# Another order of the same steps on five engines, and another assignment of products to three PSUM banks, in an audio tower on one core

## The reference

```
h = patches(x) @ W.T + b                                  # 64 x 92 x 128
q, k, v = split(layernorm(h) @ w_qkv.T)
p = softmax(q @ k.T * 64**-0.5)                           # per head, 92 x 92
a = layernorm_over_heads(einsum('bhij,hg->bgij', p, reattn_w)) * ln_g + ln_b
h = h + concat_heads(a @ v) @ w_out.T + b_out
x = layernorm(h)
c = two largest of softmax(x @ gate_w.T), scaled to sum 1, 0 elsewhere
h = h + sum_e c_e * (relu(x @ w1_e + b1_e) @ w2_e + b2_e) + relu(x @ sw1 + sb1) @ sw2 + sb2
```

## Time and profile before

| | |
|---|---|
| median of 3 runs | 638.89 us (638.68 to 639.09) |
| the profiled execution, its own time | 639.33 us |
| its span | 637.5 us |
| mean granted TensorE clock | 0.981 |
| busy: PE, DVE, ACT, POOL | 606.4, 441.2, 402.4, 368.5 us |
| setup and start, to `dots` 0 of group 0 | 24.4 us |
| iteration 0, iteration 1 | 28.9, 40.5 us |
| iterations 2 to 14 | 467.8 us, 13 of them |
| iteration 15; 16 and 17 | 33.0; 42.9 us |

### The profile page before, as it was taken

How to read it: one execution, slowest core, us unless ns; L and a number is a source line. 1 busy time by engine, 2 the same in 40 slices (tenths; PEclk the granted TensorE clock), 3 DMA queues, 4 the chain that set the end, 5 groups by cost and what they waited for, 6 DMA issues and landing times.

```text
span 637.5 us, 17017 instructions
## 1 busy us (share of the span) xinstructions
PE 606.4 (95%) x6275; PEld 529.2 (83%) x6275; DVE 441.2 (69%) x1322; ACT 402.4 (63%) x1346; POOL 368.5 (58%) x545
## 2 busy tenths in 40 slices
PE   8886889999999999999999999999999999999796
PEld 7775779898889888898889889888888889887674
DVE  5453666768777776868777776867777786867553
ACT  3466557676866667676866667675866667666400
POOL 2566437565674847565674847566683856546300
PEclk9988969999999999999999999999999999999999
DMA  6000030120303030120303021030313020020303
GB/s 231 1 27 4 22 97 25 38 97 2 110 26 108 26 105 29 32 103 1 110 26 108 25 100 35 25 111 1 109 27 108 26 81 28 15 97 2 109 2 119
DMA packets 15460, 37.43 MB, mean 59 GB/s; under 512 B 1809, under 2 KB 4241, under 8 KB 15377
## 3 DMA queue, kind: packets, MB, share of 16 engines
q1 hardware_dynamic: 15376, 36.34, 17.1%
HBM read 33.13 MB, written 3.20 MB: 57 GB/s over the span
## 4 chain that ended last, share of the span: by engine, by line
PE 75%; ACT 7%; DVE 7%; POOL 5%; issue 3%; DMA 1%; SPq 0%; ACTq 0%; POOLq 0%; DVEq 0%
PE ps_fill L414 13%; PE ps_fill L416 11%; PE ps_fill L415 11%; PE ps_mix L642 9%; PE ps_dots L630 9%; PE ps_av L650 7%; PE ps_fill L778 6%; PE ps_fill L570 4%; ACT ex L803 3%; DVE aT L1086 3%; POOL sum L1227 2%; PE ps_fill L770 2%; ACT sq L811 2%; POOL sum L1230 1%; PE ps_fill L761 1%
## 5 line engine op out<-in xcount | busy, mean ns | idle before, releaser
L803 ACT ACTIVATE ex<-ps_dots,negmax 128x92 f32<-128x92 f32 x384 | 123.7, 341 | 7.0 <-DVE negmax L1070 6.5
L1227 POOL TENSOR_TENSOR sum<-sq 92x384 f32<-92x384 f32 x64 | 64.2, 1003 | 80.3 <-ACT sq L811 79.5
L1221 POOL TENSOR_TENSOR probs<-ex,rinv 128x552 f32<-128x552 f32 x64 | 71.0, 1109 | 29.7 <-DVE rinv L1076 29.7
L642 PE MATMUL ps_mix<-mixk,probs 64*92 64x64 f32 x1536 | 79.2, 251 | 5.5 <-DVE aT L1086 5.4
L642 PEld LDWEIGHTS ps_mix<-mixk,probs 64*92 64x92 f32 x1536 | 70.7, 163 | 16.3 <-issue 10.7
L1167 DVE SCALAR_TENSOR_TENSOR act<-ps_fill,b_neg,spread 128x368 f32<-128x368 f32 x123 | 67.9, 591 | 19.9 <-PE ps_fill L416 15.1
L803 ACT ACTIVATION_READ_ACCUMULATOR ex<-ps_dots,negmax 128x1 f32 x384 | 81.4, 212 | 0.0
L630 PE MATMUL ps_dots<-xT,yT 128*64 128x92 f32 x1536 | 75.6, 249 | 5.5 <-ACT ex L803 4.9
L630 PEld LDWEIGHTS ps_dots<-xT,yT 128*64 128x64 f32 x1536 | 65.0, 139 | 11.6 <-ACT ex L803 8.8
L1086 DVE TENSOR_TENSOR aT<-ps_mix,arstd 92x384 f32<-92x384 f32 x128 | 64.9, 547 | 7.1 <-ACT arstd L821 5.2
L1244 POOL TENSOR_TENSOR xT<-xT_split_hi,xT_split_lo 128x368 f32<-128x368 f32 x16 | 15.6, 973 | 86.1 <-DVE xT_split_lo L1146 86.1
(11 more groups left out here) (190 smaller groups left out, 1566.9 us busy)
## 6 DMA issues: line engine op xcount, KB each, us to landing
spread<-weights SPq DMA_DIRECT2D x64, 368.0 KB, 5.6
xin<-in_x SPq DMA_DIRECT2D x16, 372.0 KB, 3.2
out<-fT SPq DMA_DIRECT2D x16, 184.0 KB, 1.9
act<-w_raw SPq DMA_DIRECT2D x1, 576.0 KB, 6.5
w_sb<-w_raw SPq DMA_DIRECT2D x1, 576.0 KB, 7.2
qkv<-qk_raw SPq DMA_DIRECT2D x1, 512.0 KB, 5.2
spread<-tok_raw SPq DMA_DIRECT2D x1, 256.0 KB, 3.4
spread<-wv_raw SPq DMA_DIRECT2D x1, 256.0 KB, 5.4
```

What stands on the lines that cost most here:

```text
L642: last = pe.matmul(ps_mix[0:N, half, DH * c:DH * c + DH], probs[rows, (s - 1) % 2, c, :], mixk[rows, :, :].rearrange("p g i -> p (g i)"), ...
L803: last = act.activation(ex[:, s % 2, c, :], ps_dots[:, c // HALF, o:o + N], ACT.Exp, bias=negmax[:, c:c + 1], accum_out=sums[:, s % 2, c:c ...
L1221: pool.tensor_tensor(probs[:, s % 2, :, :], ex[:, s % 2, :, :], rinv[:, s % 2, :].unsqueeze(2).broadcast_to([128, CHUNKS, N]), ALU.mult).t ...
L1227: pool.tensor_tensor(sum4[:, :, :, :], sq[:, :, 0:4, :], sq[:, :, 4:8, :], ALU.add)\
```

## The change

`ORDER_0`, `STEPS` and all three lists of `ORDERS_END` are written anew, with the same steps in each, and `BANKS` assigns the products of the steady iteration otherwise: ten of them to each bank before, nine, eleven and ten now. `layout_banks` then gives `pD` another bank too. `SETUP` has its old order (it is only laid out on fewer lines, so that line numbers from there on are smaller by one). Nothing else differs: operations, shapes, buffers and waits by kind are the same. Of the lists, which are long, only some lines stand here:

```diff
-STEPS = [('dots', 0), ('max', 0), ('av', 0), ('ev', 0), ('mix', 0), ('exa', 0), 'Z5', 'Z3', 'Z2', ('sq', 0), ('exb', 0), 'Z6',
...
+STEPS = [('mix', 0), ('dots', 0), ('sq', 0), ('max', 0), 'Z1', 'XE', 'Z0', ('exa', 0), 'Z3', ('rstd', 0), ('exb', 0),
...
-BANKS = [['Z5', 'Z6', 'Z1', 'TK', 'TH', 'V3', 'TX', 'Y5', 'Y1', 'Y0'],
- ['Z3', 'Z8', 'Z7', 'TH2', 'TX2', 'RT', 'CT', 'Y3', 'Y4', 'V0'],
- ['Z2', 'Z0', 'OP', 'Z4', 'V2', 'YF', 'Y6', 'Y2', 'Y7', 'BS']]
+BANKS = [['Z0', 'Z7', 'Z6', 'TK', 'TH', 'TX', 'Y6', 'Y7', 'Y1'],
+ ['Z3', 'Z5', 'OP', 'TH2', 'TX2', 'RT', 'YF', 'BS', 'Y4', 'Y2', 'Y3'],
+ ['Z1', 'Z4', 'Z2', 'Z8', 'V2', 'V3', 'CT', 'Y0', 'Y5', 'V0']]
...
-ORDER_0 = [('dots', 0), ('max', 0), ('exa', 0), 'prepF', ('exb', 0), ('inv', 0), 'XE', 'XO', 'shift', 'V3', ('dots', 1),
...
- ['Z1', 'Z0', 'Z8', 'T2', 'Z3', 'T4', 'T5', 'T6', 'T7', 'YF']]
...
+ORDER_0 = ['shift', 'XE', ('dots', 0), 'XO', ('max', 0), ('exa', 0), ('exb', 0), 'prepF', 'TK', 'V3', ('dots', 1), ('inv', 0),
...
+ ['Z8', 'Z3', 'Z0', 'Z1', 'T6', 'T2', 'T7', 'T4', 'T5', 'YF']]
```

More of the change, by code:

```diff
@@ L74 @@
           "av": 2, "ev": 2}
-STEPS = [('dots', 0), ('max', 0), ('av', 0), ('ev', 0), ('mix', 0), ('exa', 0), 'Z5', 'Z3', 'Z2', ('sq', 0), ('exb', 0), 'Z6',
- ('inv', 0), 'XE', ('dots', 1), ('rstd', 0), ('max', 1), ('scale', 0), 'Z8', 'Z0', 'Z1', ('exa', 1), ('mix', 1),
[5 rows of a table removed]
+STEPS = [('mix', 0), ('dots', 0), ('sq', 0), ('max', 0), 'Z1', 'XE', 'Z0', ('exa', 0), 'Z3', ('rstd', 0), ('exb', 0),
+ ('av', 0), ('scale', 0), ('inv', 0), ('ev', 0), 'Z4', 'Z5', 'Z7', 'XO', ('dots', 1), 'H0', ('av', 1), ('mix', 1),
+ ('max', 1), ('ev', 1), ('exa', 1), ('sq', 1), ('exb', 1), 'Z6', 'Z2', 'OP', ('rstd', 1), 'Z8', ('dots', 2),
+ ('inv', 1), ('max', 2), 'shift', 'TH2', ('exa', 2), ('scale', 1), 'TK', ('exb', 2), 'NH2', 'V2', ('inv', 2),
[4 rows of a table added]
 LAG = {"XE": 1, "XO": 1, "TK": 1, "TH": 1, "NH": 1, "TX": 1, "BS": 1, "V0": 1, "V2": 0, "V3": 0,
@@ L130, in present @@
     return exists(G + LAG[step], NG)
-ORDER_0 = [('dots', 0), ('max', 0), ('exa', 0), 'prepF', ('exb', 0), ('inv', 0), 'XE', 'XO', 'shift', 'V3', ('dots', 1),
[L135 to L146, removed]
[4 rows of a table removed]
+ORDER_0 = ['shift', 'XE', ('dots', 0), 'XO', ('max', 0), ('exa', 0), ('exb', 0), 'prepF', 'TK', 'V3', ('dots', 1), ('inv', 0),
+ ('mix', 1), ('max', 1), 'TH', ('exa', 1), ('sq', 1), ('exb', 1), 'V2', ('dots', 2), ('inv', 1), ('max', 2),
+ ('rstd', 1), ('scale', 1), ('exa', 2), ('mix', 2), ('exb', 2), 'NH', ('dots', 3), ('sq', 2), 'TX', ('av', 2),
+ ('inv', 2), ('rstd', 2), 'Y2', ('scale', 2), 'XS', 'Y6', 'Y0', ('mix', 3), ('max', 3), ('ev', 2), 'Y3', 'Y7',
+ ('sq', 3), ('exa', 3), 'Y5', ('exb', 3), ('inv', 3), ('rstd', 3), 'BS', ('av', 3), ('scale', 3), ('ev', 3), 'Y1',
+ 'prepG', 'Y4', 'V0']
+ORDERS_END = [[('mix', 0), ('dots', 0), ('sq', 0), ('max', 0), ('exa', 0), ('rstd', 0), 'Z0', 'Z3', ('exb', 0), 'Z1', ('av', 0),
+  ('scale', 0), ('inv', 0), ('ev', 0), 'Z7', 'H0', 'Z8', 'Z5', ('dots', 1), ('av', 1), ('max', 1), ('ev', 1),
+  ('mix', 1), ('exa', 1), ('sq', 1), 'Z2', ('exb', 1), ('inv', 1), 'OP', ('dots', 2), ('max', 2), ('rstd', 1),
[7 rows of a table added]
 def order(G):
@@ L175, in last_expert @@
     return [step for step in order(G) if step in EXPERTS][-1]
[L178 to L181, removed]
+SETUP = ['XE', 'XO', 'prepT', 'prepW', 'TK', 'TH', 'prepO', 'prepB', 'NH', 'pA0', 'pA1', 'TX', 'pM', 'Y6', 'Y3', 'Y0', 'Y7',
+ 'Y4', 'Y5', 'XS', 'Y2', 'V0', 'Y1', 'BS', 'pD', 'prepX', 'prepE']
 def nth(step, steps):
```

## The result

The changed kernel takes 645.41 us (median of 4 runs, 644.31 to 647.13), the kernel before 638.78 beside it: ratio 1.0107, 95% interval 1.008 to 1.0134. It is slower by about 1%; 629.6 was forecast. The profiled run took 644.58 us, its span is 642.8.

The account below looks back on a forecast made before the run. PE, busy 95%, was taken to bound the middle by its own instruction sequence, chains of waits the ends; -4.5 - 3.8 - 2.2 + 1.24 = -9.3, and 639.33 - 9.3 - 0.44 = 629.6 us, range 622.5 to 636.

Parts of the forecast that it names:

- Middle groups: Groups 2 to 14: PE's reordered steps take 35.67 us a group instead of 35.96, term -3.8 us, bounds -6.4 to nothing won.
- the near hand-overs: Middle groups: `TX` 0.15 late, `BS`, `mix` 2 and `mix` 0 about on time; 0.2 us a group allowed.
- a wait of `TX` of 0.1 to 0.2: Middle groups: sign expected if the forecast holds, `TX` waiting 0.1 to 0.2 us on VectorE's normalised rows.
- Rival 2: Middle groups: the loop from `mix` 3 to the next `mix` 0 becomes the bound; slower, 643 us; chance 0.13.
- Rival 3: Group 1: stops of 3.1 and 4 us prolong half clock, costing 4 to 5 us in groups 1 and 2; 634; chance 0.10.
- What was to prove me wrong: Middle groups: a group length of 36 us or more, or a regular wait of `mix` 0 on VectorE's scaling.
- Groups 0 and 1: Start: PE's gap ahead of `dots` 1 closes, stalls shift; -2.9 in group 0, -1.6 in group 1, together -4.5 us.
- Group 15: `av` 2 moves behind `mix` 3, stops ahead of `mix` 3 shrink to 1.4 us; term -2.2, bounds -3 and 0.
- Group 16: Chain from `mix` 0 through `OP`, `TX2`, `RT` to `CT` has nothing new on it; term 0.
- Group 17: Last product waits for `Z3`, which needs the second DMA piece of weights; term +1.24 us, bounds 0 and +1.6.
- the three stretches of the earlier trace: Kernel before: three stretches at granted clock 0.50, each after a PE stop of 2 us or more, given as 23.9 us.

Follow-up runs that it names:

- experiment 2: Kernel before with only GpSimd's half of `H1` (a split of two experts) moved behind the probabilities of slot 2 in the middle list; 651.74 us, ratio 1.021.
- experiment 6: Kernel before with only the new `ORDER_0`, all else including `BANKS` as before; 639.28 us, ratio 1.003.
- experiment 4: Changed kernel with `H1` directly behind `OP` in the middle list and group 15, there also `inv` 2 directly behind its exponentials; 631.52 us, ratio 0.9889.

## Right or wrong, step by step

- **Middle groups: wrong by 9.1 us, and this is the step that failed.** "I followed each hand-over with the row durations" took each duration as the instruction's own, and so counted the hand-over from the routing to `CT`, `Y6` and `mix` 3 among those that "arrive 0.3 us or more ahead of PE". The routing's duration depends on what GpSimd does in that moment: +1.57 us for `hot`, of which PE had slack for a good half and lost 0.76 a group, 13 x 0.76 = 9.9. With the collision taken away the group measures 35.63 against 35.67 forecast. Of the seven runs of products, forecast at 1.72, 1.72, 3.74, 3.15, 0.81, 7.93 and 4.66, the sixth, which holds the routing, took 8.65 in the changed kernel and 8.03 without the collision, and each of the others lies within 0.1 in both. So price and order of PE's steps were right, and the allowance of 0.2 for the near hand-overs. The order has one change of tile shape more, at 0.10 us. The Trainium skill (TensorEngine Tiling (Array Packing), section Key Properties) says that changing the tiling mode drains TensorE; by that alone the middle would have become slower. Here the extra change was covered by what else went, 35.63 against 35.96. One sign that I named, a wait of `TX` of 0.1 to 0.2, shows as no stop in either kernel.
- **It could have been read before.** In the kernel before, `shift_l`, as small as its neighbours of 0.18 us, took 0.52 us in groups 1 to 14 and 1.30 in group 15. Its end in group 5, 225.37, lies 0.03 behind the end of GpSimd's probabilities (224.23 + 1.11):

```profile
224.85 0.52 DVE L1034 TENSOR_TENSOR shift_l<-logit,top 128x24 f32<-128x24 f32 x1
```
```profile
224.23 1.11 POOL L1221 TENSOR_TENSOR probs<-ex,rinv 128x552 f32<-128x552 f32 x1 [0.41 <-DVE rinv L1076]
```

- **Rivals.** None of mine was this. Rival 2 said that a group more than 0.42 us above 35.96 makes the kernel slower, and the group came 0.43 above, but by another mechanism: there `mix` 0 waits for the scaling, and here it never does in groups 2 to 16. Its sum did not hold either, since the other terms, -5.5 there, came to nothing. Rival 3 had the clock cost time in groups 1 and 2; it cost time in groups 16 and 17. What was to prove me wrong, a group of 36 or more, did.
- **Groups 0 and 1: the mechanism was right, and part of the size was luck.** `dots` 0 at 25.22 (24.8 forecast), `mix` 2 at 37.12 behind a stop of 1.94 (37.0 and 2.2), then the clock fell, group 1 at 50.49 (50.4), no stop ahead of `dots` 1 of group 0, two stops of over 3 us in group 1 (3.08 and 3.53). Group 0 gave -2.8 (-2.9 forecast) and group 1 -3.3 (-1.6), together -6.1 instead of -4.5. But the run before had spent 23.9 us at half clock up to there, and this one 13.7. Seven profiled kernels with these lists start group 2 between 87.28 and 92.25, and three with the old list of group 1 between 91.21 and 93.80: the two spreads overlap. Where the time at half clock is the same, 13.6 to 13.7 us, it is 91.21 with the old lists (experiment 2) against 87.28 to 88.29 in four kernels with the new ones. So the order gives 3 to 4 us, and the rest of the -6.1 is the clock's. Group 0's share of 2.9 is not its list's alone (experiment 6).
- **Group 15: the term -2.2 came out as -0.4**, the same collision; without it -1.7 (33.40 against 35.07). That it was not worse was luck: in four of the five profiles with the collision the clock fell there too, and the term would be +1.9 or more (experiment 4).
- **Group 16: the term 0 was wrong, +3.3.** "Nothing new on it" looked at the chain and not at what keeps PE busy beside it: three products instead of five between `av` 0 and `av` 1, stops of 0.45 and 1.78 us instead of 0.46 and 0.77, and the clock fell. With five again, and a different order around them, 24.35 us at 1.00.
- **Group 17: the mechanism was right.** The last product starts 0.66 us after the first expert, which the second DMA piece released; 9.61 against 9.11 forecast. What I left out: PE stands 2.81 us ahead of the last product, the clock falls inside it, and the end grows by 1.5 (10.53 against 8.99). The clock fell there in three of the six profiled kernels with this list.
- **Range and chances.** 622.5 to 636 missed by 9 us, because no term allowed an instruction to change its duration, and the ends were taken at full clock. The span is 14.6 us above the forecast: 9.1 in the middle, 1.8 in group 15, 3.3 in group 16, 2.0 behind it, less 1.6 at the start. One sum in the prediction is off and carries nothing: the lengths of the three stretches of the earlier trace rows add up to 23.75, not 23.9.

## What to carry to other kernels

When an order changes, check what runs on GpSimd while VectorE does instructions with two inputs in SBUF: such an instruction can last as long as the reads on GpSimd (0.18 us became 1.75 and 2.82 here), and the profile books that as busy time without a wait. A small instruction that is longer than its equals of the same shape is the sign, and it is there before any change. Where products are moved away from a wait, count what is left to keep PE busy there, since a stop can bring the half clock on what follows, here for 3.4 to 10.2 us at a time. One profiled run does not settle such a price, because the same stop brought the half clock in some runs and not in others.

## What was not expected of the hardware

VectorE waits for more than one GpSimd instruction. With copies of 0.79 us each it was held 1.52 us, until both had ended; in group 15 it was held 2.82, through a split of 1.74 and probabilities of 1.10 behind it. The Trainium skill (SBUF — State Buffer, section SBUF: two separate sides) gives the ports that VectorE and GpSimd share to whichever instruction starts first, for the whole of that instruction. By that alone one would expect VectorE to come in between the two. Here the measurement decides: back-to-back reads on GpSimd kept it out. By the trace the second one starts 0.04 us before the first ends (584.02 against 582.32 + 1.74), so there was no gap between them; whether that is the reason was not tried. A reduction with one input ran at its 0.18 us beside GpSimd's sum (292.94 in group 7 of the changed kernel).
